# Moving the two layer norms' subtract and multiply from GpSimd to VectorE in an AdaLN, mLSTM and mixture-of-experts kernel

## The reference

```
layernorm(x) = (x - mean) / sqrt(var + 1e-5)          # over the 128 features
h = layernorm(x) * (1 + ca) + sa
x = x + ga * mLSTM(h)        # RMS norm, q/k/v/gates, 512-step gated recurrence, output matrix, + h
h = layernorm(x) * (1 + cb) + sb
x = x + gb * MoE(h)          # 8 experts, top 2 by softmax of the router, 128 -> 256 -> 128, relu
```

## Time and profile before

| | |
|---|---|
| time, median of 3 runs | 385.44 us (383.62 to 387.99) |
| the profiled execution, its span | 385.9 us; it is the time that its rows add up to, no other time of it is given |
| TensorE busy | 343.8 us (89%) |
| VectorE busy | 281.8 us (73%) |
| ScalarE busy | 227.7 us (59%) |
| GpSimd busy | 185.6 us (48%) |
| chain that ended last | TensorE 61%, VectorE 23%, issue 6%, ScalarE 3%, GpSimd 3% |

### The profile page before, as it was taken

The page is one execution under the profiler, slowest core; times in us unless marked ns, Lnnn a source line. Parts: engine busy times, 40 slices in busy tenths (PEclk is TensorE's granted clock), DMA queues, the critical chain, the costliest instruction groups (busy, mean ns, idle before and its releaser), DMA issues.

```text
span 385.9 us, 6042 instructions
## 1 busy us (share of the span) xinstructions
PE 343.8 (89%) x1744; PEld 275.5 (71%) x1744; DVE 281.8 (73%) x786; ACT 227.7 (59%) x412; POOL 185.6 (48%) x180
## 2 busy tenths in 40 slices
PE   2926988999899989998999989998999899887995
PEld 2814976778687858886687868786887678665783
DVE  3787457689767986689668876897668976765664
ACT  1420232777476848586567747684857685674673
POOL 7794072148543764276326833384505641573240
PEclk9975698999899998999899989998999999998998
DMA  4840000000000000000000000000000001000000
GB/s 117 268 115 2 0 1 2 0 3 0 0 3 27 0 0 0 27 0 0 0 27 0 0 0 0 27 0 0 0 27 2 0 0 31 0 0 2 27 2 27
DMA packets 8965, 7.10 MB, mean 18 GB/s; under 512 B 1195, under 2 KB 7510, under 8 KB 8950
## 3 DMA queue, kind: packets, MB, share of 16 engines
q1 hardware_dynamic: 8722, 6.78, 6.1%
q0 software_dynamic: 64, 0.07, 0.1%
q10 hardware_dynamic: 164, 0.07, 0.1%
HBM read 4.82 MB, written 2.10 MB: 18 GB/s over the span
## 4 chain that ended last, share of the span: by engine, by line
PE 61%; DVE 23%; issue 6%; ACT 3%; POOL 3%; DMA 1%; SPq 1%; DVEq 0%; POOLq 0%
PE bank L956 7%; PE bank L958 6%; PE bank L957 6%; PE bank L984 5%; PE bank L974 5%; PE bank L975 5%; PE bank L926 5%; PE bank L994 3%; DVE hg L763 3%; PE bank L911 3%; PE bank L859 2%; PE bank L933 2%; DVE hg_lo L774 2%; DVE top_d L652 2%; DVE m_row L741 2%
## 5 line engine op out<-in xcount | busy, mean ns | idle before, releaser
L424 POOL TENSOR_TENSOR hg_lo<-hg,hg_hi 128x512 fp32r<-128x512 f32 x69 | 88.8, 1289 | 89.5 <-ACT hg_hi L494 89.5
L476 ACT ACTIVATE hid<-bank,cols 128x512 f32<-128x512 f32 x128 | 87.3, 682 | 69.4 <-PE bank L958 69.2
L763 DVE TENSOR_TENSOR hg<-hid,bank 128x512 f32<-128x512 f32 x128 | 86.7, 681 | 53.0 <-PE bank L994 32.7
L494 ACT ACTIVATE hg_hi<-hg 128x512 fp32r<-128x512 f32 x128 | 79.6, 622 | 9.0 <-DVE hg L763 8.8
L956 PE MATMUL bank<-h_hi,w_hi 128*128 (+1 forms) x128 | 58.9, 460 | 0.0
L984 PE MATMUL bank<-hg_lo,w_hi 128*128 128x512 f32 x128 | 52.6, 411 | 1.0 <-DVE hg_lo L774 0.9
L974 PE MATMUL bank<-hg_hi,w_hi 128*128 128x512 f32 x128 | 52.7, 412 | 0.0
L975 PE MATMUL bank<-hg_hi,w_lo 128*128 128x512 f32 x128 | 52.0, 407 | 0.0
L957 PE MATMUL bank<-h_hi,w_lo 128*128 (+1 forms) x128 | 51.5, 403 | 0.0
L958 PE MATMUL bank<-h_lo,w_hi 128*128 (+1 forms) x128 | 51.3, 401 | 0.0
L393 POOL TENSOR_SCALAR var_eps<-mv 128x4 f32<-128x4 f32 x16 | 4.5, 278 | 87.6 <-DVE mv L555 87.6
(11 more groups left out here) (162 smaller groups left out, 626.1 us busy)
## 6 DMA issues: line engine op xcount, KB each, us to landing
out_dram<-x_all SPq DMA_DIRECT2D x8, 256.0 KB, 2.3
w_raw<-in_L_ffn_W_dram SPq DMA_DIRECT2D x1, 1024.0 KB, 9.1
x_all<-in_L_attn_x_dram SPq DMA_DIRECT2D x2, 256.0 KB, 4.2
wmod_sb<-in_L_wmod_dram SPq DMA_DIRECT2D x1, 384.0 KB, 4.9
vo_raw<-in_L_attn_Wv_dram POOLq DMA_DIRECT2D x1, 32.0 KB, 2.8
qk_raw<-in_L_attn_Wq_dram ACTq DMA_DIRECT2D x1, 32.0 KB, 2.7
vo_raw<-in_L_attn_Wo_dram POOLq DMA_DIRECT2D x1, 32.0 KB, 3.4
qk_raw<-in_L_attn_Wk_dram ACTq DMA_DIRECT2D x1, 32.0 KB, 3.1
```

Of the source, the lines that this page charges most:

```text
L424: g.tensor_tensor(hg_lo[k][:, :], hg[k][:, :], hg_hi[k][:, :].bitcast(fp32), ALU.subtract).then_inc(s_lo_pool, 1)
L476: a.activation(hid[n % 4][:, :], up_bank[n % 2][:, :], ACT.Relu, bias=cols[:, R_B1 + n:R_B1 + n + 1]).then_inc(s_hid, 1)
L494: a.activation(hg_hi[k][:, :], hg[k][:, :], ACT.Copy).then_inc(s_hghi, 1)
L763: v.tensor_tensor(hg[k][:, :], hid[k][:, :], gate_bank[n // NU % 2][:, :], ALU.mult).then_inc(s_hg, 1)
```

## The change

GpSimd's `norm` keeps the power alone. VectorE adds the epsilon itself, behind its own aggregate, and a new function `norm_apply` subtracts the mean and multiplies by the reciprocal deviation in one instruction per 128 tokens, four per norm. It stands behind the opening weights for the very first norm, at the end of step 7 for norm 1, and at the end of step 8 for norm 0 of the row ahead. The semaphore between GpSimd's subtraction and multiplication is gone.

```diff
-            def norm(k, b, first=False):
-                wait_apart(pool, s_mv[k], b + 1)
-                g.tensor_scalar(var_eps[k][:, :], mv[k][:, :, 1], LN_EPS, None, ALU.add).then_inc(s_ve[k], 1)
-                if k == 0 and not first:
-                    wait_apart(pool, s_xT, b)
-                g.tensor_tensor(xn[k][:, :, :], row(x_all, b).rearrange("p (j d) -> p j d", j=NT),
-                                bcast(mv[k][:, :, 0], D), ALU.subtract).then_inc(s_xc[k], 1)
-                pool.wait_ge(s_ve[k], b + 1)
+            def norm(k, b):
+                wait_apart(pool, s_ve[k], b + 1)
                 g.tensor_tensor(rstd[k][:, :], var_eps[k][:, :], minus_half[:, :], ALU.pow).then_inc(s_rs[k], 1)
-                pool.wait_ge(s_xc[k], b + 1)
-                wait_apart(pool, s_rs[k], b + 1)
-                g.tensor_tensor(xn[k][:, :, :], xn[k][:, :, :], bcast(rstd[k][:, :], D), ALU.mult).then_inc(s_xn[k], 1)
...
             def norm_aggr(k, b):
...
                 last.then_inc(s_mv[k], 1)
+                wait_apart(dve, s_mv[k], b + 1)
+                v.tensor_scalar(var_eps[k][:, :], mv[k][:, :, 1], LN_EPS, None, ALU.add).then_inc(s_ve[k], 1)
+
+            def norm_apply(k, b, first=False):
+                if k == 0 and not first:
+                    wait_apart(dve, s_xT, b)
+                wait_apart(dve, s_rs[k], b + 1)
+                for j in range(NT):
+                    last = v.tensor_scalar(xn[k][:, j, :], x_all[:, bass.ds(b * T + j * P, P)], mv[k][:, j, 0:1],
+                                           rstd[k][:, j:j + 1], ALU.subtract, ALU.mult)
+                last.then_inc(s_xn[k], 1)
...
             v.tensor_copy(woutT[:, :], bank[3][0:DH, 0:D]).then_inc(s_proj, 1)
+            norm_apply(0, 0, first=True)
...
                         norm_aggr(0, b + 3)
+                    if end and t == 7:
+                        norm_apply(1, m1)
+                    if ahead and t == 8:
+                        norm_apply(0, b + 3)
```

More of the change, by code:

```diff
@@ L224, in adaln_mlstm_moe_kernel @@
         s_rs = [sem(f"s_rs{k}") for k in range(2)]
-        s_xc = [sem(f"s_xc{k}") for k in range(2)]
         s_xn = [sem(f"s_xn{k}") for k in range(2)]
@@ L424, in body @@
                         g.tensor_tensor(hg_lo[k][:, :], hg[k][:, :], hg_hi[k][:, :].bitcast(fp32), ALU.subtract).then_inc(s_lo_pool, 1)
-            norm(0, 0, first=True)
+            norm(0, 0)
             g.memset(sel, 0.0).then_inc(s_sel0, 1)
```

## The result

The median is 398.8 us (397.8 to 399.9, 4 runs) against 384.7 us (383.6 to 388.0, 4 runs) on the same chip: a ratio of 1.032, 95% interval 1.027 to 1.038. A run's time is 1.8 us longer than the span of its rows (399.7 against 397.9 for the one profiled here).

What follows compares the result with a forecast made beforehand. VectorE's unbroken chain to vs, for which TensorE already waits, was taken to bound the full turns. Five turns +14.5, clock -2.7, end turns -4.6 gave +7.2 on 385.9, so 393 us; range 382 to 398.

Steps and rivals of the forecast that it cites:

- second turn: GpSimd's multiplication right ahead of the rms power goes, no split beside it yet: -1.0 us (0 to -1.6).
- What bounds it: VectorE's chain from kk to vs has no hole and TensorE waits at its end; additions go straight to the turn.
- The lateness: End of vs in a full turn: 2.9 us late, bounds 0.3 and 3.9; +14.5 us over five turns.
- The price of four: Four new 128x128 VectorE instructions: 0.52 us taken, from a 512-element cast; upper end 0.79.
- steps 3 and 4: Full turn, after the second application: GpSimd's h_lo holds rms to 218.78, its next hg_lo holds the copy into vs to 219.97.
- var_eps: Epsilon addition on VectorE, 16 times 0.15 us plus about 0.1 wait: cost 0; without cover 2.5 us in five turns.
- That VectorE is not held: Rival, 20%: second application takes the port before GpSimd or needs none; vs about 0.3 us late, total 383.
- One hold fewer: Rival, 25%: GpSimd's hg_lo comes a little later, the copy into vs slips through; 1.7 us a turn, total 390 or 388.
- The power holds too: Rival, 10%: GpSimd's power keeps the port, so both applications are held; 3.9 us a turn, total 401.
- The clock: Full turns: half-speed fall moves to the vs wait, m_row wait mostly goes; -2.7 us, ends -4.5 and +3.5.
- The range: Total time: 382 to 398 us, taking in the unheld case, leaving out the power case and far tails.
- The ends: First, second, sixth and seventh turns, where GpSimd's passes stand on the path: sum -4.6 us (-1 to -5.7).

Runs made afterwards that it cites:

- e4_imm: Changed kernel with constants 0.0 and 1.0 as the two scalars of the application; 395.8 us, ratio 1.023.
- e5_cut: Changed kernel with GpSimd's hg_lo of step 9 cut to 8 of its 512 columns; 389.0 us, ratio 1.011.
- e8_step7: Changed kernel with the application of norm 0 moved up from the end of step 8 to the end of step 7; 387.7 us, ratio 0.992.
- e11_stop: Kernel before, with TensorE's residue matmul of step 10 also waiting for the square of rms, about 0.5 us; 386.4 us, ratio 0.997.
- e12_stop2: Kernel before, with TensorE's residue matmul of step 10 also waiting for zo, a longer stop; 386.8 us, ratio 1.004.
- e1_norm0: Changed kernel with only norm 0 applied by VectorE (step 8), norm 1 on GpSimd as before; 399.0 us, ratio 1.039.
- e2_norm1: Changed kernel with only norm 1 applied by VectorE (step 7), norm 0 on GpSimd as before; 383.9 us, ratio 0.995.
- e3_late0: Changed kernel with the application of norm 0 moved from the end of step 8 to the end of step 18; 382.9 us, ratio 0.995.

## Why the prediction was right, and where it was not

| term, us | forecast | profiled |
|---|---|---|
| opening and first turn | -1.7 | -2.75 |
| second turn | -1.0 | +1.63 |
| five full turns, wait for `vs` | +14.5 | +13.7 |
| five full turns, clock and wait for `m_row` | -2.7 | +0.9 |
| sixth turn | -0.3 | -0.28 |
| seventh turn and the rest | -1.6 | -1.24 |
| sum | +7.2 | +12.0 |

*What bounds it* was right: what makes VectorE's chain longer goes to the turn, and GpSimd's splits decide how much. *The lateness* of `vs` was forecast at 2.9 us and is 2.88, but by luck: two of its steps were wrong and cancelled. The price of four was 1.02, not 0.52: the nearest row that I took, the 512-element cast, reads no scalar from SBUF. And at that price steps 3 and 4 don't happen: `rms` and the copy are free, and the second application carries both holds itself. `e4_imm` has the forecast's price, and step for step the forecast's holds. `var_eps` cost nothing that shows: `kk` starts right behind ScalarE's `qq` as before (218.31, when `qq` ends at 218.27; 211.03 and 211.00 before).

*That VectorE is not held* (rival, 20%) is excluded by the 3.10 us and by `e5_cut`. *One hold fewer* did not occur in any full turn. *The power holds too* is excluded: it started at 220.57 beside the first application, which took its bare 1.02. The whole-instruction hold of the Trainium skill (SBUF — State Buffer, "Who interferes with whom") is not what these rows show for the power; for the splits they agree with it (held to 224.44 and to 226.22).

*The clock* is the step that failed. Half of it came as written: the fall to half speed moved to the wait for `vs`, and the wait for `m_row` went in all five turns, 6.2 us in sum. But I let the half-speed stretch keep its 3.4 us, with 1.6 us of slip, and it doubled to 6.8, 6.3 of it work: the busy time of the five turns rose by 7.1 us. Forecast -2.7, measured +0.9. This is 3.6 of the 4.8 us that were missed; the smaller `vs` term takes 0.8 back. Why the stretch doubled is open; `e5_cut` shows that the same wait can come with 6.8 us, with 3.4 or with none.

*The range* was too narrow by its own terms. Its lower end takes the best of each (385.9 + 14.5 - 4.5 - 5.7 = 390.2), but the worst of each gives 385.9 + 14.5 + 3.5 - 1.0 = 402.9, not 398; and its ends of -1 to -5.7 add up to -1.9 to -5.7. The prediction also set the span of 385.9 beside a median of times, which are 1.8 us longer than their spans: by that the profiled execution was 0.6% slower than the median of 385.44, not 0.1%.

*The ends* make up the other 2.0. The first turn gained 2.75, more than its 0 to 2.2 (its rms power starts at 17.8 us against 19.4), the sixth and the rest went as forecast in sign and roughly in size. The second turn did not. `vs` ends 13.4 us after the turn's start instead of 14.1, so that 0.65 of the forecast's 1.0 came, but TensorE's clock in the turn is 0.82 instead of 0.94. Whether that belongs to the change is not settled. With VectorE applying both norms in step 7 and 8 it was 28.7, 27.2 (`e5_cut`) and 27.5 us (`e4_imm`), and with both in step 7 28.6 (`e8_step7`); with the code of before, 27.05, 26.8 (`e11_stop`) and 29.1 (`e12_stop2`); with the opening on VectorE and this turn on GpSimd, 25.97 three times, at 1.00. The last are the shorter ones; the others differ by less than they vary. One norm on VectorE did not lengthen it: 26.0 us with norm 0 alone (`e1_norm0`), 25.5 with norm 1 alone (`e2_norm1`).

## What to carry to other kernels

Work that is moved to another engine is priced by its place, not by its length: four such instructions of 1.0 us lengthened the chain by 2.8 us behind `hg_lo`, by 1.0 half a step earlier (1.23 for both norms, less 0.21 for the other), and by 0.2 where they took the place of other holds. Look for a place where the receiving engine already waits for the engine that bounds the turn, and put only that part there; here the whole loss went with one moved call. When a wait on TensorE grows, do not assume that the half-speed stretch with it keeps its size: read its length from the rows, in several turns, and give the term a range that holds both none and twice.

## What was not expected of the hardware

- The same `tensor_scalar` of 128x128 fp32 took 0.135 us with constants and 0.255 with two scalars read from SBUF, from start to start.
- A stop of 1.4 us on TensorE that ended 8.6 us before the end of the `m_row` wait came with a clock of 1.00 behind that wait in four full turns of five, where the kernel before has 0.50 for 3.4 us; with a stop of 0.5 us in the same place four turns of five kept the slow stretch. With the longer stop a full turn ran 0.4 us shorter with 1.0 us more idle time.
- The granted clock of a turn takes few values: in the four turns of the loop that are alike, TensorE is busy 38.0 to 38.3 us at 1.00, 39.5 to 39.8 at 0.96 and 40.8 to 41.2 at 0.92. In the traces of `before`, `after`, `e3_late0`, `e5_cut`, `e8_step7` and the two stops, these are turns with no half-speed stretch, with one of 3.4 us and with one of 6.8. The kernel before ran from 382.4 to 391.9 us over the chips used here; one execution of it was traced, so how much of that is such steps is not shown.
